# Cross-attention and routed feed-forward on one core: the routing weight loads on ScalarE's DMA queue, the weight differences in the middle head groups, the last reciprocals ahead of VectorE's closing work

## The chip, the core and the metric

The kernel runs on one core of a Trainium2 chip. Such a core has TensorE (PE, matrix products; its weight loads are listed apart as PEld), VectorE (DVE), ScalarE (ACT) and GpSimd (POOL), and SyncE (SP), which here only issues DMA transfers. Each engine works through its own instructions in order; they meet only at semaphores. DMA transfers are put into a queue by the engine that issues them: SP's queue and ScalarE's queue are the two that this kernel uses. SBUF is the on-chip memory, PSUM the banks that TensorE writes.

The metric is the time on the device in microseconds (us) of the whole program. Lower is better.

## The reference, cut to what matters

The inputs are x, 8 batches of 512 tokens by 512, and a context of 1601 rows by 128 for each batch, of which the causal mask leaves the first 512. Layer one is cross attention with 16 heads of 32:

```
x = x + Attention(layernorm(x), ctx, Wq, Wkv, Wout)     # causal softmax over keys
```

Layer two is a mixture of 8 experts whose weights are chosen per token and per output column:

```
logits = (h @ router_w.T + router_b).reshape(T, O, E)    # h = layernorm(x), O = 512, E = 8
w, sel = top_k(softmax(logits), 2);  w = w / sum(w)
c[t, e] = sum of w over the columns that chose e
x = x + sum_e c[t, e] * (h @ expert_w[e].T + expert_b[e])
```

Only differences of logits matter for the choice, so the kernel multiplies with 7 weight differences, router e minus router 0 (e = 1 to 7), rather than with 8 weights.

## The kernel before

All products of consequence are taken in three parts: each float32 operand is split into a high part (made on ScalarE, a rounding copy) and a low part (full minus high, on VectorE or GpSimd), and TensorE adds high*high, high*low and low*high. In the profile these are lines L264, L265 and L266.

The program has three stages. **Attention** walks over 8 batches; each has 4 head groups c = 0 to 3 of 4 heads, so 32 groups n = 0 to 31, and each group has 8 steps v = 0 to 7 (two heads and one block of keys each). TensorE runs `scores` of a later group (L608, L611), VectorE takes the row maxima (`maxima`, L1253), TensorE turns the maxima (L620), ScalarE and VectorE split them (`hi_shift` L949, `lo_shift` L1262), SP copies the two parts into rows 96 and 97 of the stacked operand `qk_st` (`rows`, L329), and `shifted_scores` (L638) repeats the score product with the maxima taken off. ScalarE takes the exponential (L997), GpSimd masks the diagonal block (L1696) and adds the blocks of keys up in `acc` (L1683, L1688), and TensorE forms the values (L651) and the sums (L663, L671); the sums of group n come in step v = 1 of group n + 1. In steps 1 to 3 VectorE takes their reciprocals (L1273), in step 4 it multiplies (`scaled`, L1279); ScalarE and GpSimd split the result into `oT_h` (L956) and `oT_l` (L1641). `project_out` for the batch before runs in groups c = 1 and 2; VectorE adds the residual (L1284) and SP stores it (L367). `stack` (L343) copies queries and keys of the group three ahead into `qk_st` by 12 transfers.

The **last batch** (groups 28 to 31) has no next batch to prepare. In it the routing weights are loaded into SBUF space that the projections no longer use, on SP's queue (L405, L407, L410; `w_raw`, 1 MB each; router 0 goes to slot 5), and VectorE subtracts router 0 in place (`diff_router`, L1358, 128x2048). The table PREPARED says in which (c, v) step each of the first five differences is taken. BIAS_STEPS does the same for five small instructions that split the router bias (7 partitions). SELECTED places GpSimd's work on `bias_sel` (L1727, L1732); its first step waits until the stacks of all 32 groups have landed.

Then comes the **tail of attention** (`epilogue` on each engine): the last output projection (`project_last`, 12 products of three for the three earlier groups, 4 of three for the last), whose last part waits for group 31's scaled outputs, the layer norm of the first token block (`stats2`, L1196; `deviation` on GpSimd, L1650 and L1652; `norm2`, L1210), its transposes (`turn_block`, L821) and their split (`hi_block` L1034, `lo_block` L1386), the last residual adds (L1289), and the split of the routing weights (`hi_router` L924 on ScalarE, `lo_router` L1398 on VectorE). Two differences (5 and 6) are taken on GpSimd (L1750), after `w_zero` and their weights have been loaded.

**Routing** then does 32 blocks of 128 tokens with 7 products of 12 matmuls each, and **experts** 32 blocks with 8. In the first expert block the weights are still being split (`hi_expert` L1093, `lo_expert` L1566). `put_c` (L1556 to L1561) lays out the coefficients of a block in `c_pad` and `turn_c` (L867) transposes them on TensorE, for block t + 1 after expert 3 of block t. `expert` (L1577) adds an expert's product to `xb` and so frees its PSUM bank.

The order on every engine is the order of the code: there is no scheduler. In the closing stretch the waits between engines set it.

## Time and profile before

| | |
|---|---|
| runs before | 2114.68, 2108.54 and 2114.58 us; median 2114.58 |
| profiled execution | 2109.79 us, its span 2108.1 us |
| TensorE busy | 2026.7 us, 96% of the span |
| VectorE, ScalarE, GpSimd busy | 70%, 48%, 40% |
| mean granted TensorE clock | 0.988 |

The profile's times are microseconds from the start of the span. A row of a timeline gives start, duration, engine, line, operation, output and inputs, the count of instructions merged in it, and in brackets the idle time before it with what ended it. A row of waits gives who waited for whom, the total, the number of waits and the longest. A row of the chain gives start, duration and what it is. A row of windows gives the stretch and its length, busy time of PE, PEld, DVE, ACT and POOL with counts, the granted TensorE clock as a share of full speed, the DMA share and GB/s. ("SPq" is SP's issuing of a transfer, not the transfer.)

Where the rows lie: group 29 (c = 1 of the last batch) runs from 622 to 642 us, group 30 from 648 to 666, group 31 from 666 to 685, the tail from 685 to 706, then routing until 1391.9 and the experts.

### The profile page before, as it was taken

What the parts mean: (1) busy time and instruction counts of PE and PEld (TensorE: products, weight loads), DVE (VectorE), ACT (ScalarE), POOL (GpSimd) and SP (SyncE); (2) the same over time, 40 slices, a digit from 0 to 9 for tenths busy, and PEclk for the clock granted to TensorE, in tenths of its full rate; (3) what the DMA queues carried; (4) which work ended last, traced back from release to release, by engine and by line L of the source; (5) the groups of instructions that cost most, each with busy time, mean ns of one, the idle gap of its engine ahead of it and who ended that gap; (6) DMA issues with size and microseconds to landing.
All of it is one profiled execution on the core that took longest, in us unless ns stands there. A gap on an engine that the chain in (4) does not pass through costs nothing.

```text
span 2108.1 us, 31621 instructions
## 1 busy us (share of the span) xinstructions
PE 2026.7 (96%) x10334; PEld 1564.7 (74%) x10384; DVE 1476.0 (70%) x2532; ACT 1005.4 (48%) x2030; POOL 852.7 (40%) x987
## 2 busy tenths in 40 slices
PE   4899999999997899999999999999999999999999
PEld 3666767766764677777777777778888888888887
DVE  4667767767666667777778777657877878778533
ACT  1454454454443346767676776733433334333300
POOL 3677677667667334435344345202311113111100
PEclk8999999999998999999999999999999999999999
DMA  5444544544544545455455355472322222322110
GB/s 154 104 106 125 141 116 115 144 117 112 129 108 165 185 161 204 161 193 184 162 177 204 150 190 188 156 269 81 109 95 75 78 92 93 107 80 75 60 40 31
DMA packets 99214, 275.82 MB, mean 131 GB/s; under 512 B 13435, under 2 KB 14480, under 8 KB 95030
## 3 DMA queue, kind: packets, MB, share of 16 engines
q1 hardware_dynamic: 94518, 216.16, 32.4%
q10 hardware_dynamic: 4608, 58.72, 8.1%
q8 instruction: 27, 0.44, 0.1%
q14 instruction: 61, 0.50, 0.1%
HBM read 131.67 MB, written 92.27 MB: 106 GB/s over the span
## 4 chain that ended last, share of the span: by engine, by line
PE 86%; DVE 7%; DMA 2%; issue 2%; POOL 1%; SPq 1%; ACT 1%; DVEq 0%; POOLq 0%; ACTq 0%
PE pair L264 21%; PE pair L266 20%; PE pair L265 20%; PE pair L608 4%; PE ps L264 3%; PE ps L651 3%; PE pair L638 3%; DVE nmax L1253 3%; PE ps L265 2%; PE ps L266 2%; PE pair L844 2%; PE pair L611 2%; DVE o_sb L1273 1%; PE ps L671 1%; DVE qk L1239 1%
## 5 line engine op out<-in xcount | busy, mean ns | idle before, releaser
L264 PE MATMUL pair<-w_h,hT 128*128 128x512 f32 x1920 | 797.4, 415 | 1.8 <-DVE w_l L1398 1.6
L266 PE MATMUL pair<-w_h,hT 128*128 128x512 f32 x1920 | 751.5, 391 | 0.0
L265 PE MATMUL pair<-w_l,hT 128*128 128x512 f32 x1920 | 747.6, 389 | 0.0
L1769 POOL TENSOR_TENSOR logits<-logits,second 128x512 f32<-128x512 f32 x224 | 298.4, 1367 | 608.1 <-DVE second L1456 607.8
L266 PEld LDWEIGHTS pair<-w_h,hT 128*128 128x128 f32 x1920 | 360.6, 188 | 80.3
L265 PEld LDWEIGHTS pair<-w_l,hT 128*128 128x128 f32 x1920 | 361.7, 188 | 74.6
L264 PEld LDWEIGHTS pair<-w_h,hT 128*128 128x128 f32 x1920 | 363.3, 189 | 69.6 <-issue 0.6
L997 ACT ACTIVATE pT<-pair,zero 128x1024 f32<-128x1024 f32 (+3 forms) x256 | 202.7, 793 | 258.9 <-PE pair L638 251.9
L1577 DVE SCALAR_TENSOR_TENSOR xb<-pair,c_now,xb 128x512 f32<-128x512 f32 x256 | 191.9, 750 | 189.2 <-PE pair L266 182.9
L1253 DVE TENSOR_REDUCE nmax<-pair 128x2 f32<-128x1024 f32 (+3 forms) x256 | 209.0, 816 | 150.4 <-PE pair L611 147.4
L1696 POOL TENSOR_SCALAR_AFFINE_SELECT pT<-pT 128x256 f32<-128x256 f32 x256 | 109.0, 427 | 147.0 <-ACT pT L997 146.3
L608 PE MATMUL pair<-qk_st 96*128 96x256 f32 (+3 forms) x512 | 135.5, 347 | 25.0 <-DVE nmax L1253 20.5
L1650 POOL TENSOR_TENSOR rstd<-moments,eps 128x1 f32<-128x1 f32 x64 | 33.0, 516 | 302.9 <-DVE moments L1206 268.3
L1510 DVE SCALAR_TENSOR_TENSOR scrap<-ps,w 128x512 bf16<-128x512 f32 x224 | 153.2, 684 | 0.0
L608 PEld LDWEIGHTS pair<-qk_st 96*128 96x128 f32 x512 | 88.7, 193 | 86.6 <-DVE nmax L1253 39.9
L1504 DVE SCALAR_TENSOR_TENSOR ps<-logits,ps 128x512 f32<-128x512 f32 x192 | 133.3, 694 | 17.0 <-DVE scrap L1510 0.5
L1061 ACT ACTIVATE over<-over 128x512 f32<-128x512 f32 x224 | 141.7, 633 | 7.0
L1058 ACT ACTIVATE junk<-over 128x512 bf16<-128x512 f32 x224 | 141.5, 632 | 7.1
L638 PE MATMUL pair<-qk_st 98*128 98x256 f32 (+3 forms) x512 | 135.1, 347 | 5.9 <-DMA qk_st<-nm_l 5.9
L1085 ACT ACTIVATE w<-tree 128x512 f32<-128x512 f32 x32 | 20.3, 633 | 238.0 <-DVE tree L1458 238.0
L1688 POOL TENSOR_TENSOR acc<-acc,pT 128x512 f32<-128x512 f32 (+1 forms) x124 | 128.8, 1039 | 10.3
L1053 ACT ACTIVATE over<-logits 128x512 f32<-128x512 f32 x224 | 129.6, 623 | 0.5
(164 smaller groups left out, 2877.4 us busy)
## 6 DMA issues: line engine op xcount, KB each, us to landing
logits<-lg_all ACTq DMA_DIRECT2D x32, 1792.0 KB, 7.8
qk_st<-qk SPq DMA_DIRECT2D x384, 128.0 KB, 2.3
lg_all<-ev_a SPq DMA_DIRECT2D x32, 768.0 KB, 6.0
lg_all<-ev_b SPq DMA_DIRECT2D x32, 768.0 KB, 3.2
xb<-x SPq DMA_DIRECT2D x64, 256.0 KB, 3.1
hT_all<-hT SPq DMA_DIRECT2D x32, 512.0 KB, 3.6
hT<-hT_all SPq DMA_DIRECT2D x32, 512.0 KB, 3.6
xt<-in_x SPq DMA_DIRECT2D x8, 1024.0 KB, 5.5
```

The lines of the kernel that those rows point to most:

```text
L264: pe.matmul(dst, lh, rh, start=start, stop=False)
L265: pe.matmul(dst, lh, rl, start=False, stop=False)
L266: return pe.matmul(dst, ll, rh, start=False, stop=stop)
L608: pe.matmul(s_ps[:, j, 0:w], qk_st[c][0:STACK, 0, hh, i * P:w], qk_st[c][0:STACK, 1, hh, 0:w], start=True, stop=False)
L638: mm = pe.matmul(dst[:, j, 0:w], qk_st[c][0:STACK + SHIFT_ROWS, 1, hh, kb * P:(kb + 1) * P], qk_st[c][0:STACK + SHIFT_ROWS, 0, hh, kb * P: ...
L997: act.activation(pT[kb][:, pair:pair + 2, :], src[:, :, 0:S - kb * P], ACT.Exp, bias=zero[:])\
L1058: act.activation(junk[:], over[j][:], ACT.Sign, accum_out=sign_sum[:, i, e:e + 1])\
L1061: act.activation(over[j][:], over[j][:], ACT.Tanh, scale=0.5, accum_out=tanh_sum[:, i, e:e + 1]).then_inc(s["first_step"], 1)
L1253: dve.tensor_reduce(nmax[:, c % 2, at:at + QB + 1:QB], s_ps[:, :, 0:(i + 1) * P], AX_X, ALU.max, negate=True)\
L1510: dve.scalar_tensor_tensor(scrap[:, e % 2, :], taken_ps[e % 2], 1.0, w2[:], ALU.min, ALU.mult, accum_out=c_taken[:, i, e - 1:e]).then_inc( ...
L1577: dve.scalar_tensor_tensor(xb[i][:], l_ps[e % 4], c_now[i][:, e:e + 1], xb[i][:], ALU.mult, ALU.add).then_inc(s["acc"], 1)
L1769: pool.tensor_tensor(logits[t % 2][:, e - 1, :], logits[t % 2][:, e - 1, :], second[:], ALU.subtract)\
```

## The change

The six routing weight loads and the two bias loads leave SP's queue. ScalarE issues them instead, one in each of six steps of the table LOADED, (0,6), (0,7), (1,0), (1,1), (1,3) and (1,5), behind that step's exponential. The five differences on VectorE move from steps (2,6), (2,7), (3,0), (3,5) and (3,6) to (1,2), (1,4), (2,2), (2,4) and (3,5), and the bias steps shift to other steps. In VectorE's epilogue the reciprocals and the scaling of group 31 stand first. On TensorE the transposes of the first token block come after two of the last four projection products, no longer before the four. `put_c` for block 1 runs before the first expert block instead of after its first expert.

```
@@ sync, last batch @@
-                    if not more and c == 0:
-                        sp.wait_ge(s["q_mm"], NB)
...
-                        sp.dma_start(w_raw[:, EARLY], r_v[:, 0]).then_inc(s["diff0_in"], 16)
-                        for e in range(1, EARLY - 1):
-                            sp.dma_start(w_raw[:, e - 1], r_v[:, e]).then_inc(s[f"diff{e}_in"], 16)
-                    if not more and c == 1:
-                        for e in range(EARLY - 1, EARLY + 1):
-                            sp.dma_start(w_raw[:, e - 1], r_v[:, e]).then_inc(s[f"diff{e}_in"], 16)
@@ tensor, epilogue @@
-                turn_block(0, 0)
                 for i in range(QB):
                     project_last(i, KC - 1)
+                    if i == 1:
+                        turn_block(0, 0)
@@ scalar @@
+            LOADED = ((0, 6), (0, 7), (1, 0), (1, 1), (1, 3), (1, 5))
+
+            def load_router(k):
+
+                if k == 0:
+                    act.wait_ge(s["q_mm"], NB)
+                    act.wait_ge(s["k_mm"], NB)
+                    act.wait_ge(s["v_mm"], B * QB)
+                    act.dma_start(w_raw[:, EARLY], r_v[:, 0]).then_inc(s["diff0_in"], 16)
+                else:
+                    act.dma_start(w_raw[:, k - 1], r_v[:, k]).then_inc(s[f"diff{k}_in"], 16)
+                if k == 1:
+                    act.dma_start(bias_raw[0:ND, :], router_b[1:NE, :]).then_inc(s["bias_in"], 16)
...
@@ vector @@
-            PREPARED = ((2, 6), (2, 7), (3, 0), (3, 5), (3, 6))
-            BIAS_STEPS = ((1, 4), (1, 5), (1, 6), (1, 7), (2, 5))
+            PREPARED = ((1, 2), (1, 4), (2, 2), (2, 4), (3, 5))
+            BIAS_STEPS = ((1, 5), (1, 6), (1, 7), (2, 0), (2, 6))
@@ vector, epilogue @@
                 dve.memset(bias_rows[:], 0.0).then_inc(s["bias_zero"], 1)
+                for v in DIVIDED:
+                    reciprocals(NB - 1, KC - 1, v, last_d_ps)
+                scaled(NB - 1, KC - 1, last_o_ps)
                 stats2(0, 0)
                 mean_variance(0, 0, "ln2")
                 lo_router(0)
                 norm2(0, 0)
-                for v in DIVIDED:
-                    reciprocals(NB - 1, KC - 1, v, last_d_ps)
-                scaled(NB - 1, KC - 1, last_o_ps)
                 lo_router(1)
@@ vector, experts @@
             put_c(0, 0)
+            dve.wait_ge(s["c_ok"], 2)
+            dve.wait_ge(s["c_put"], 1)
+            put_c(1, 1)
...
-                    if e == 0 and t + 1 < NT:
+                    if e == 0 and 0 < t < NT - 1:
```

VectorE in group 29 (c = 1 of the last batch), from the reciprocals of step 1 on, before; `o_sb` are the outputs of the group before, `xr` the residual, `nmax` the maxima:

```order
L1273 RECIPROCAL o_sb_89<-ps 128x176
L1253 TENSOR_REDUCE nmax<-pair 128x2
L1273 RECIPROCAL o_sb_89<-ps 128x176
L1284 TENSOR_TENSOR xr<-ps,xr 128x512
L1253 TENSOR_REDUCE nmax<-pair 128x2
L1273 RECIPROCAL o_sb_89<-ps 128x160
L1253 TENSOR_REDUCE nmax<-pair 128x2
L1279 TENSOR_TENSOR o_sb_89<-ps,o_sb_89 128x512
L1407 TENSOR_TENSOR bias_raw<-bias_raw,bias_zero_row 7x512
L1253 TENSOR_REDUCE nmax<-pair 128x2
```

The same place of the changed kernel, whose line numbers are four higher; `w_raw` are the routing weights:

```order
L1277 RECIPROCAL o_sb_89<-ps 128x176
L1257 TENSOR_REDUCE nmax<-pair 128x2
L1277 RECIPROCAL o_sb_89<-ps 128x176
L1362 TENSOR_TENSOR w_raw<-w_raw 128x2048
L1288 TENSOR_TENSOR xr<-ps,xr 128x512
L1257 TENSOR_REDUCE nmax<-pair 128x2
L1277 RECIPROCAL o_sb_89<-ps 128x160
L1257 TENSOR_REDUCE nmax<-pair 128x2
L1283 TENSOR_TENSOR o_sb_89<-ps,o_sb_89 128x512
L1362 TENSOR_TENSOR w_raw<-w_raw 128x2048
L1257 TENSOR_REDUCE nmax<-pair 128x2
```

One difference stands ahead of the residual add, a second one in the place of the first bias step, ahead of the last maxima. Group 30 gets two at the same places, with nothing taken out there.

VectorE's tail, from the scaling of group 30 to the second `lo_router`, before (`xb` is the first token block):

```order
L1279 TENSOR_TENSOR o_sb_91<-ps,o_sb_91 128x512
L1358 TENSOR_TENSOR w_raw<-w_raw 128x2048 x2
L1362 MEMSET bias_rows 128x256
L1196 BN_STATS stats<-xb_103 128x6
L1205 MEMSET turn 128x1
L1206 BN_AGGR moments<-stats 128x2
L1398 TENSOR_TENSOR w_l<-w_raw,w_h 128x2048
L1210 TENSOR_SCALAR xb_103<-xb_103,moments,rstd 128x512
L1273 RECIPROCAL o_sb_89<-ps 128x176 x2
L1273 RECIPROCAL o_sb_89<-ps 128x160
L1279 TENSOR_TENSOR o_sb_89<-ps,o_sb_89 128x512
L1398 TENSOR_TENSOR w_l<-w_raw,w_h 128x2048
```

The same tail of the changed kernel:

```order
L1283 TENSOR_TENSOR o_sb_91<-ps,o_sb_91 128x512
L1362 TENSOR_TENSOR w_raw<-w_raw 128x2048
L1366 MEMSET bias_rows 128x256
L1277 RECIPROCAL o_sb_89<-ps 128x176 x2
L1277 RECIPROCAL o_sb_89<-ps 128x160
L1283 TENSOR_TENSOR o_sb_89<-ps,o_sb_89 128x512
L1200 BN_STATS stats<-xb_103 128x6
L1209 MEMSET turn 128x1
L1210 BN_AGGR moments<-stats 128x2
L1402 TENSOR_TENSOR w_l<-w_raw,w_h 128x2048
L1214 TENSOR_SCALAR xb_103<-xb_103,moments,rstd 128x512
L1402 TENSOR_TENSOR w_l<-w_raw,w_h 128x2048
```

The reciprocals and the scaling of group 31 now stand ahead of the statistics, and one difference fewer stands ahead of both.

## Rows read from the trace of the kernel before

**Rows 1.** The waits of PE from 600 to 760 us, the five longest.
```profile
PE pair L264 <- POOL oT_l L1641: 6.8, 1, 6.8
PE pair L638 <- DMA qk_st<-nm_l: 5.9, 1, 5.9
PE ps L671 <- POOL acc L1688: 2.3, 1, 2.3
PE ps L651 <- POOL pT L1696: 2.0, 1, 2.0
PE ps L684 <- POOL pT L1696: 1.8, 1, 1.8
```

**Rows 2.** The timeline of SP, last batch.
```profile
631.50 1.89 SPq L407 DMA_DIRECT2D w_raw<-in_routerT  x3
633.44 2.71 SPq L367 DMA_DIRECT2D x<-xr  x1
```

**Rows 3.** The chain of waits, from 600 to 760 us.
```profile
633.44 11.56 DMA x<-xr
```

**Rows 4.** The timeline of PE, last batch and tail.
```profile
632.65 0.50 PE L264 MATMUL ps<-wo_h,oT_h 128*128 128x512 f32 x1 [0.73 <-DVE xr L1284]
...
652.61 0.83 PE L671 MATMUL ps<-acc,ones 128*32 128x384 f32 x8
...
673.19 1.50 PE L671 MATMUL ps<-acc,ones 128*32 128x384 f32 x8 [2.30 <-POOL acc L1688]
...
679.25 0.73 PE L638 MATMUL pair<-qk_st 98*128 98x256 f32 x4
...
685.24 0.50 PE L264 MATMUL pair<-wo_h,oT_h 128*128 128x512 f32 x1
...
700.97 0.77 PE L264 MATMUL pair<-wo_h,oT_h 128*128 128x512 f32 x1 [6.78 <-POOL oT_l L1641]
...
706.16 0.58 PE L264 MATMUL pair<-w_h,hT 128*128 128x512 f32 x1
```

**Rows 5.** The window of 5 us behind PE's idle time ahead of group 30.
```profile
645.00:650.00 5.00, 1.99 (x5) 1.62 (x6) 0.00 (x0) 0.73 (x1) 1.53 (x3) 0.50 0.56 151
```

**Rows 6.** The timeline of POOL, last batch and tail.
```profile
631.95 0.85 POOL L1727 MEMSET bias_sel<- 128x896 bf16 x1 [7.09 <-DMA qk_st<-qk]
...
645.89 0.72 POOL L1688 TENSOR_TENSOR acc<-acc,pT 128x256 f32<-128x256 f32 x1
...
661.30 1.28 POOL L1688 TENSOR_TENSOR acc<-acc,pT 128x512 f32<-128x512 f32 x1
...
663.48 3.34 POOL L1688 TENSOR_TENSOR acc<-acc,pT 128x512 f32<-128x512 f32 x1
...
690.12 2.15 POOL L1650 TENSOR_TENSOR rstd<-moments,eps 128x1 f32<-128x1 f32 x1 [4.40 <-DVE moments L1206]
```

**Rows 7.** The timeline of DVE, last batch and tail.
```profile
635.04 0.95 DVE L1407 TENSOR_TENSOR bias_raw<-bias_raw,bias_zero_row 7x512 f32<-7x512 f32 x1
...
663.40 2.27 DVE L1358 TENSOR_TENSOR w_raw<-w_raw 128x2048 f32<-128x2048 f32 x1
...
689.12 0.70 DVE L1196 BATCH_NORM_STATS2 stats<-xb 128x6 f32<-128x512 f32 x1 [5.37 <-DMA xb<-x]
...
693.39 3.38 DVE L1273 RECIPROCAL o_sb<-ps 128x176 f32<-128x176 f32 x3
...
712.99 5.58 DVE L1210 TENSOR_SCALAR xb<-xb,moments,rstd 128x512 f32<-128x512 f32 x1 [0.72 <-POOL rstd L1652]
```

**Rows 8.** The timeline of PE, first expert block.
```profile
1405.67 0.47 PE L867 MATMUL ps<-ident,c_pad 128*128 128x128 f32 x1 [2.39 <-DVE c_pad L1561]
...
1415.97 0.47 PE L264 MATMUL pair<-w_h,hT 128*128 128x512 f32 x1 [0.17 <-DVE xb L1577]
```

**Rows 9.** The timelines of SP and DVE, first expert block.
```profile
1405.53 0.38 SPq L487 DMA_DIRECT2D w_raw<-in_expertT  x1
...
1412.87 2.29 DVE L1566 TENSOR_TENSOR w_l<-w_raw,w_h 128x2048 fp32r<-128x2048 f32 x1 [3.73 <-ACT w_h L1093]
```

More of the change, by code:

```diff
@@ L310, in over_batches @@
             epilogue()
+        r_v = routerT.rearrange("(c p) e o -> p e c o", p=P)
         block = ctx.enter_context(nc.Block())
@@ L394, in body @@
                         load_x(b + 2)
-                    if not more and c == 0:
-                        sp.wait_ge(s["q_mm"], NB)
-                        sp.wait_ge(s["k_mm"], NB)
-                        sp.wait_ge(s["v_mm"], B * QB)
-                        sp.dma_start(bias_raw[0:ND, :], router_b[1:NE, :]).then_inc(s["bias_in"], 16)
-                        sp.dma_start(bias_zero_row[0:ND, :], router_b[0:1, :].broadcast_to([ND, O]))\
-                            .then_inc(s["bias_in"], 16)
-                        sp.dma_start(w_raw[:, EARLY], r_v[:, 0]).then_inc(s["diff0_in"], 16)
-                        for e in range(1, EARLY - 1):
-                            sp.dma_start(w_raw[:, e - 1], r_v[:, e]).then_inc(s[f"diff{e}_in"], 16)
-                    if not more and c == 1:
-                        for e in range(EARLY - 1, EARLY + 1):
-                            sp.dma_start(w_raw[:, e - 1], r_v[:, e]).then_inc(s[f"diff{e}_in"], 16)
             def load_block(t, i, name):
@@ L448, in epilogue @@
                     sp.wait_ge(s[f"x1_out{k}"], B * QB // 2 * 16)
-            r_v = routerT.rearrange("(c p) e o -> p e c o", p=P)
             e_v = expertT.rearrange("(c p) e o -> p e c o", p=P)
@@ L924, in hi_router @@
                 act.activation(w_h[:, k], w_raw[:, k], ACT.Copy).then_inc(s["fw_hi"], 1)
+            LOADED = ((0, 6), (0, 7), (1, 0), (1, 1), (1, 3), (1, 5))
[9 more added lines that the diff above has]
+                    act.dma_start(bias_raw[0:ND, :], router_b[1:NE, :]).then_inc(s["bias_in"], 16)
+                    act.dma_start(bias_zero_row[0:ND, :], router_b[0:1, :].broadcast_to([ND, O]))\
+                        .then_inc(s["bias_in"], 16)
             def hi_weight(dst, src, name):
@@ L1007, in body @@
                             hi_of(n + AHEAD, QH, "q", 1)
+                        if last and (c, v) in LOADED:
+                            load_router(LOADED.index((c, v)))
                         if c == 0 and more:
```

## The prediction

> **What bounds the kernel now.** I read the page's busy times first: TensorE is busy 96% of the span. In routing and experts nothing but its own matmuls matters, so the change can act only on the few stretches where it waits. The list of its waits around the end of attention shows them [rows 1]: 6.8 us for GpSimd's `oT_l`, 5.9 for the rows of maxima, 2.3 and 2.0 for GpSimd's sums and masks, 1.8 for a mask again; together 18.8 us. Then the timelines, to see what stands behind each wait, and the windows for TensorE's clock: in the 5.9 us wait it falls to 0.50, the lower of its two levels (1.2 GHz) [rows 5], and after the two waits for GpSimd eight matmuls take 1.50 us that took 0.83 in the group before [rows 4].
>
> Each wait's cause is one row further back. The 5.9 us: SP has put four 1 MB weight loads ahead of the residual store; the store, issued at 633.44, lands 11.56 us later [rows 2, 3], SP waits for it before it reloads that buffer, and only then, at 645, the rows of group 30 can go. The 2.3 and 2.0: a VectorE difference (2.27 us) starts at 663.40, GpSimd's add at 663.48 takes 3.34 us, and the same add without it took 1.28 [rows 6, 7]. So a difference holds GpSimd up by 2.06 us. The 6.8: group 31's reciprocals start at 693.39 [rows 7], though their sums are done by 685.24 [rows 4]; ahead of them in VectorE's order stand the statistics, whose token block arrives at 689.12, a `lo_router` and a `norm2`.
>
> **Group 29: the loads leave SP's queue.** The store now meets no weight loads in its own queue, and the rows of maxima go out when they are ready. The 5.9 us wait goes, and with it the slow clock behind it. What is late next is GpSimd. It waits for the last stack until 631.95 and is then busy without a break until its last add ends at 645.89 + 0.72 = 646.6 [rows 6]. Two differences now fall into that stretch: 2 x 2.06 = 4.1, so 650.7. The stack shares the DMA engines with ScalarE's loads; I add 0.5 us (bounds: 0, and 11.6, the store's landing, if it stood behind them all). The sums of group 29 then start at 651.2 instead of 652.61 [rows 4]. VectorE's own delay is 2.27 and 2.27 - 0.95 for the bias step that made room [rows 7], 3.6 us, plus some waiting for GpSimd; it puts TensorE at those sums at about 649, covered by GpSimd's 651.2. Term: **-1.4 us**. ScalarE's eight issues cost some half a microsecond each (1.89 us for three on SP [rows 2]) and stand in gaps of about 1 to 2 us between exponentials; if its queue pushed back as in the store's 2.71 us [rows 2], it could be 2 us in one step, which GpSimd's lag hides as well.
>
> **Group 30: two differences in the middle.** VectorE has no idle time from step 1 to step 5 there; TensorE already waited 0.73 us for the residual add in the same step of group 29 [rows 4]. So both differences lie on the path: 2 x 2.27 = 4.5, and 0.5 for differences that find a GpSimd instruction running. Bounds: 4.5 and, if each waits for a whole 1.28 us add, 7.1. **+5.0 us**. In return none stands at the end of group 30: the waits of 2.0 and 2.3 [rows 1] go. **-4.3 us**. The sums of group 30 start at 673.19 - 1.4 + 5.0 - 4.3 = 672.5.
>
> Here the Trainium skill bears (SBUF — State Buffer, Who interferes with whom): a VectorE instruction with two inputs in SBUF and a GpSimd instruction that reads SBUF exclude each other entirely, and whichever issued first goes on. The trace agrees on both sides: 3.34 against 1.28 for GpSimd, and a 5.58 us `norm2` on VectorE that met GpSimd's long subtraction [rows 6, 7]. By that rule a moved difference costs the same wherever GpSimd is busy; if the two merely shared bandwidth, group 29 would give some 2 us more.
>
> **Group 31.** Before, the clock was low from 673.19: eight L671 took 1.50 against 0.83 at full speed [rows 4], and the 6.06 us from there to 679.25 are about 3.6 at full clock. **-2.4 us**. One difference is left in step 5; it still holds GpSimd's last masks, so most of the 1.8 us wait stays: **-0.1**. The last projection starts at 685.24 - 3.2 = 682.0.
>
> **The tail.** All from there. Reciprocals 682.1 to 685.5 (3.38 [rows 7]), scaling to 686.2. The token block arrives three microseconds earlier too, as its issue hangs on group 30's `oT_l`: 686.2. Statistics and variance take 0.9 us, GpSimd's deviation 2.15 beside a `lo_router` [rows 6] and a short power 0.55: 689.9; only then comes GpSimd's `oT_l`, 1.3 us: 691.2. TensorE has worked on the other 36 matmuls to 690.3 and waits 0.9 us, not 6.8. At full clock 12 matmuls take 2.8 instead of the 5.2 us from 700.97 to 706.16 [rows 4]. But the transposes now stand between them (0.6), and behind them the split of the block on ScalarE and VectorE and a residual add, 0.9 us beyond TensorE's own end. Routing starts at 691.2 + 2.8 + 0.6 + 0.9 = 695.5, not 706.16: -10.7. Its fifth product hangs on VectorE's `norm2` and `lo_router`, and these on the residual adds, which end 9.8 us earlier. So attention gives **-9.8 us** in all, of which the tail has 6.6.
>
> **The early put_c.** TensorE waits 2.39 us for `c_pad` at 1405.67 and then runs slowly, 8 matmuls at 0.43 instead of 0.23 us apart: 4.0 us in all (the two paces are those of the 12 matmuls above). Both go. But expert 7 starts at 1415.97 behind VectorE's `xb` add, which stands behind the last `lo_expert` (1412.87 + 2.29), whose weights were only requested at 1405.53 [rows 8, 9]. None of that moves. The 4.0 us turn into a wait ahead of expert 7, and a wait so long brings the lower clock behind it, now uncovered: 8 x 0.2 = **+1.7 us** (bounds 0 and 2.5).
>
> **Sum.** -9.8 + 1.7 = -8.1 us. Against the profiled execution's own 2109.8 this is 2101.7; against the median 2114.6 it is 2106.5. The runs of before differ by 6 us among themselves, so I take a value between, 2104.
>
> **The rivals.**
> *A. The loads hold up the last stack.* ScalarE's first four loads are issued while SP stacks group 31. If the DMA engines serve them first, the stack lands late by about the 11 us that four loads took [rows 3], GpSimd's `bias_sel` step waits for it [rows 6], and its backlog sets group 29's sums us for us: -8.1 + 11 = +3, 2112.8 from the profiled time and up to 2117.5 from the median, slower than before. It decides from 8.1 us of delay on. For it: the store's 11.56 us. Against: the store stood in the same queue. The Trainium skill (DMA: Bandwidth & Descriptors, Queues, rings and completion order) says that each DMA engine takes turns between queues, packet by packet; by it the stack would only share the engines with the loads, and rival A would come to almost nothing. No row of this trace shows two such queues at once.
> *B. The middle costs more.* If each of group 30's two differences first waits for a GpSimd add (2 x 1.28), and TensorE's stalls of 3 us there bring the lower clock (2 x 1.6), the sum is -8.1 + 5.8 = -2.3: 2107.5, or 2112 from the median. For it: VectorE has no slack; against: a slow TensorE is partly hidden behind VectorE there.
> *C. GpSimd is no hindrance and the clock holds.* Then group 29 gives 2.6 us more, and expert 7's wait costs nothing (1.7): -12.4, 2097.4. For it: waits of 1.8 and 2.0 us left the clock alone; against: the rows of the lock.
>
> **Chances.** Forecast 0.48 (its own range -5 to -11), B 0.25, C 0.20, A 0.07. Less than 0.3%, 6.3 us, can't be told from no change here. Faster by more: four fifths of the forecast's, nearly all of C's and a little of B's, 0.6. Within: the rest of the forecast's, most of B's, most of A's, 0.35. Slower by more: 0.05. The range 2096 to 2112 takes in C with a microsecond to spare and B from either base.
>
> **What would show it.** In the changed profile: no wait for `qk_st<-nm_l`; a wait of 1 to 3 us at the sums of group 29 for GpSimd; new waits of 2 to 3 us for the residual add (L1288) and the maxima (L1257); the 2.0 and 2.3 us waits for GpSimd gone at the end of group 30; the wait for `oT_l` about 1 us; routing's first product 10 to 11 us earlier; a 4 us wait ahead of expert 7 and none for `c_pad`. Wrong would be: a late GpSimd memset of `bias_sel` (A), or group 30's sums later than in the kernel before (B).

## The result, and the profile after

The forecast was 2104 us (2096 to 2112), 8.1 us less than before. Measured: a median of 2116.63 us (2112.47 to 2119.66, 17 runs) against 2112.77 us of the kernel before (2108.54 to 2114.75, 17 runs). The ratio is 1.002, with a 95% interval of 1.0013 to 1.0028: slower, by some 4 us. The prediction was wrong in sign and in size.

The profiled execution took 2119.66 us, its span 2117.9 against 2108.1 before. From its page, busy times and then the DMA queues (packets, MB, share of 16 engines' span):

```profile
PE 2037.6 (96%) x10334; PEld 1571.8 (74%) x10384; DVE 1479.5 (70%) x2532; ACT 1005.8 (47%) x2030; POOL 849.9 (40%) x987
...
q1 hardware_dynamic: 91322, 209.84, 31.2%
q10 hardware_dynamic: 7804, 65.04, 9.0%
```

The loads did move: ScalarE's queue (q10) carries 65.04 MB instead of 58.72.

**4.6 of the 9.8 us between the two spans have nothing to do with the change.** The sums of group 27 (the last ones before any changed code) start at 608.09 us before and at 612.70 after. The windows where this arises, of the kernel after (columns: stretch, length, busy time of PE, PEld, DVE, ACT and POOL, then TensorE's granted clock):

```profile
100.00:110.00 10.00, 10.00 (x66) 6.60 (x65) 5.68 (x10) 3.77 (x5) 5.16 (x14) 0.70 0.65 150
110.00:120.00 10.00, 8.96 (x45) 5.53 (x43) 7.34 (x12) 6.51 (x11) 8.50 (x10) 0.83 0.05 11
```

The kernel before has a granted clock of 1.00 in both windows, in the same code. So all that follows is measured from group 27's sums. Where the milestones stand from there, in us, each read from the first matmul of its kind in TensorE's timeline (in step 1 of a group TensorE sums the group before), the memset from GpSimd's:

| milestone | before | after | p1 | p2 | p3 | p4 | q3 | r1 | r2 | r3 | s1 |
|---|---|---|---|---|---|---|---|---|---|---|---|
| GpSimd's memset of `bias_sel` | 23.9 | 32.8 | 32.8 | 31.3 | 32.1 | 31.2 | 28.3 | 31.6 | 24.1 | 29.2 | 22.5 |
| group 28's sums | 17.9 | 20.0 | 21.2 | 21.4 | 22.5 | 20.1 | 17.9 | 22.3 | 17.9 | 17.9 | 17.9 |
| group 29's sums | 44.5 | 47.9 | 46.9 | 45.6 | 51.2 | 47.8 | 44.2 | 49.4 | 45.0 | 42.9 | 44.2 |
| group 30's sums | 65.1 | 70.5 | 67.5 | 67.6 | 71.9 | 73.2 | 64.8 | 73.4 | 65.5 | 65.8 | 65.0 |
| last projection | 77.1 | 79.8 | 79.9 | 79.6 | 81.2 | 82.5 | 77.0 | 82.7 | 77.6 | 78.4 | 78.3 |
| routing, product 1 | 98.1 | 93.3 | 100.1 | 93.1 | 102.1 | 96.0 | 90.5 | 96.2 | 91.2 | 91.9 | 91.8 |
| routing, product 5 | 112.8 | 113.0 | 114.8 | 112.8 | 116.8 | 115.6 | 110.2 | 112.6 | 107.6 | 108.3 | 104.2 |
| routing, product 6 | 115.8 | 118.3 | 117.8 | 118.1 | 119.8 | 119.9 | 115.7 | 116.9 | 112.7 | 112.7 | 109.8 |
| experts | 783.8 | 786.3 | 785.8 | 786.0 | 787.8 | 787.8 | 783.6 | 784.9 | 780.7 | 780.7 | 779.2 |
| expert block 2 | 810.9 | 815.5 | 813.1 | 812.1 | 816.6 | 813.3 | 812.4 | 815.6 | 808.3 | 808.0 | 805.6 |
| end | 1500.0 | 1505.2 | 1502.2 | 1501.1 | 1505.6 | 1502.4 | 1501.5 | 1504.6 | 1497.3 | 1497.1 | 1494.5 |

(p1 to s1 are the experiments below.) The loss from group 27 on is 5.2 us, near the 3.9 us of the medians. TensorE's waits in the end of attention, kernel after, 600 to 770 us (total, times, longest), which answer to [rows 1]:

```profile
PE ps L264 <- DVE xr L1288: 5.9, 2, 2.9
PE ps L807 <- DVE xb L1214: 3.1, 1, 3.1
PE ps L605 <- DVE nmax L1257: 2.6, 2, 1.5
PE pair L830 <- ACT w_h L910: 2.2, 1, 2.2
PE pair L623 <- DMA qk_st<-nm_l: 2.1, 1, 2.1
PE pair L264 <- DVE w_l L1402: 1.4, 1, 1.4
...
PE pair L264 <- POOL oT_l L1648: 0.8, 1, 0.8
```

The 6.8 us for `oT_l` are 0.8, the 5.9 us for rows are gone, and the 2.3 and 2.0 us for GpSimd in [rows 1] are no longer among the long ones. But others came: two of 2.9 us for the residual add; 2.1 us for rows, one group earlier than the 5.9 had been; and three in routing's first block (L807, L830, `w_l`), 6.7 us together, where the kernel before waits 0.37 and 1.61.

The issues of ScalarE's and SP's queues around the last stack (start, length):

```profile
623.33 0.45 ACTq L920 DMA_DIRECT2D w_raw<-in_routerT  x1
625.31 0.39 ACTq L922 DMA_DIRECT2D w_raw<-in_routerT  x1
...
630.18 0.39 ACTq L922 DMA_DIRECT2D w_raw<-in_routerT  x1
632.12 0.41 ACTq L922 DMA_DIRECT2D w_raw<-in_routerT  x1
637.10 0.37 ACTq L922 DMA_DIRECT2D w_raw<-in_routerT  x1
```
```profile
624.27 0.57 SPq L331 DMA_DIRECT2D qk_st<-nm_h  x1
624.88 0.59 SPq L331 DMA_DIRECT2D qk_st<-nm_l  x1
625.64 8.07 SPq L345 DMA_DIRECT2D qk_st<-qk  x12
641.56 0.35 SPq L369 DMA_DIRECT2D x<-xr  x1
647.48 0.33 SPq L365 DMA_DIRECT2D xr<-in_x  x1
```

What came of it, first in the chain of waits, then on GpSimd, then on TensorE:

```profile
633.11 12.26 DMA qk_st<-qk
```
```profile
645.49 0.85 POOL L1734 MEMSET bias_sel<- 128x896 bf16 x1 [13.71 <-DMA qk_st<-qk]
```
```profile
629.41 0.73 PE L623 MATMUL pair<-qk_st 98*128 98x512 f32 x2 [2.08 <-DMA qk_st<-nm_l]
...
641.59 0.60 PE L264 MATMUL ps<-wo_h,oT_h 128*128 128x512 f32 x1 [2.93 <-DVE xr L1288]
...
669.49 0.80 PE L264 MATMUL ps<-wo_h,oT_h 128*128 128x512 f32 x1 [2.92 <-DVE xr L1288]
```

The last piece of the stack, issued at 633.11, lands 12.26 us later. GpSimd's memset comes 32.8 us behind group 27's sums, where it was 23.9 [rows 6]: 8.9 us late, and I had given it 0.5. The residual store now stands behind no load in its own queue, and SP still goes on only 5.9 us after it (641.56 to 647.48; 11.56 in [rows 3]); the median of these stores is 2.1 us.

**This one profile shows the middle milder than most.** Nine kernels here (after, p1 to p4, q2, q4, q5, r1) issue the loads at these early steps, and each has a wait of 1.97 to 2.36 us for group 29's rows. In after and p4 the granted clock stayed at 1.00 behind it; in the other seven it fell to 0.50. Their group 28's sums stand at 21.2 to 22.5, those of after and p4 at 20.0 and 20.1, and those of every kernel without early loads at 17.9 (s1 17.8). The mean of the nine is 21.5, so this place costs 3.6 us in the mean and not 2.1.

### The profile page after: what moved, and what is told of

Read it like the earlier page. It is cut to its first block, busy times and chain, and to the rows that moved or that the text cites. A ratio compares the mean times of both kernels' runs of the same rounds, so it can differ in the third digit from the quotient of the medians.

```text
span 2117.9 us, 31622 instructions
## 1 busy us (share of the span) xinstructions
PE 2037.6 (96%) x10334; PEld 1571.8 (74%) x10384; DVE 1479.5 (70%) x2532; ACT 1005.8 (47%) x2030; POOL 849.9 (40%) x987
## 3 DMA queue, kind: packets, MB, share of 16 engines
q1 hardware_dynamic: 91322, 209.84, 31.2%
q10 hardware_dynamic: 7804, 65.04, 9.0%
## 4 chain that ended last, share of the span: by engine, by line
PE 86%; DVE 7%; DMA 2%; issue 2%; POOL 1%; SPq 1%; ACT 0%; DVEq 0%; POOLq 0%; ACTq 0%
PE pair L264 21%; PE pair L266 20%; PE pair L265 20%; PE pair L593 4%; PE ps L636 3%; PE ps L264 3%; PE pair L623 3%; DVE nmax L1257 3%; PE ps L265 2%; PE ps L266 2%; PE pair L830 2%; PE pair L596 2%; DVE o_sb L1277 1%; DVE qk L1243 1%; PE ps L656 1%
```

## The experiments

Each ratio is that to the kernel before on the same chip, with its 95% interval. First the loads were made alone, and then each other part undone by itself. Diffs are against the kernel after, where nothing else is said.

### p1: the loads alone

The kernel before, with the loads on ScalarE and nothing else of the change.

```diff
-PREPARED = ((1, 2), (1, 4), (2, 2), (2, 4), (3, 5))
-BIAS_STEPS = ((1, 5), (1, 6), (1, 7), (2, 0), (2, 6))
+PREPARED = ((2, 6), (2, 7), (3, 0), (3, 5), (3, 6))
+BIAS_STEPS = ((1, 4), (1, 5), (1, 6), (1, 7), (2, 5))
...  and the tail and put_c as in the kernel before
```

> The kernel before with one part of the change, the loads on ScalarE's queue. Distances are counted from the sums of group 27 (before: sums of group 29 at +44.5, last projection at +77.2, routing at +98.1). Theory (loads and last stack share the DMA engines, GpSimd's bias_sel waits for the stack): the wait of 5.9 us for the rows goes, but bias_sel starts 7 to 9 us later, group 29's sums stand at +47 to +49, the last projection at +80, and the kernel is 2 to 5 us slower than before. Rival (only the moved differences cost anything): bias_sel on time, sums of group 29 at +39 to +41, the kernel 5 us faster than before.

Measured: 2112.89 us, ratio 1.0008 [0.9997, 1.0019]: by the time alone no difference from before, where 2 to 5 us were expected. What follows is read from its profile. The loads alone bring GpSimd's memset to 32.8 us and group 28's sums to 21.2 instead of 17.9:

```profile
626.52 0.73 PE L623 MATMUL pair<-qk_st 98*128 98x512 f32 x2 [1.97 <-DMA qk_st<-nm_l]
...
643.96 1.28 PE L636 MATMUL ps<-pT,v_sb 128*32 128x512 f32 x8 [2.22 <-POOL pT L1699]
...
655.98 0.43 PE L636 MATMUL ps<-pT,v_sb 128*32 128x128 f32 x8 [1.90 <-POOL pT L1699]
```

So the new wait for group 29's own rows and the late stack both belong to the loads. The 5.9 us wait is gone, and waits for GpSimd's masks stand in its place. The last projection comes 2.8 us later than before. Three kernels (before, r2, s1) share all code up to that point and have it at 77.1, 77.6 and 78.3, mean 77.7; p1 and p2 have 79.9 and 79.6. So the early loads cost about 2.1 us in the mean of profiles.

### p2: the old middle

After, with the two tables `PREPARED` and `BIAS_STEPS` of before (the diff of p1's first four lines).

> The changed kernel with the differences and bias steps back at their old places, all else as changed. Theory: group 29's sums stay at +47 to +49 (changed kernel +47.9), since the stack is late without the differences too; group 30's waits for GpSimd of 2.0 and 2.3 us come back; the last projection at +79 to +81; time within 2 us of the changed kernel. Rival (the moved differences are the whole loss): sums of group 29 at +40, time 7 us under the changed kernel.

Measured: 2114.48 us, ratio 1.0013 [1.0003, 1.0024]. The last projection is at 79.6, that of after at 79.8. But six kernels here (after, p3, p4, q4, q5, r1) share all code up to that point, and theirs lies at 79.8 to 82.9, mean 81.9. p1 and p2, with the old middle behind early loads, have 79.9 and 79.6. The moved differences thus cost 2.2 us in the mean of profiles, and a single profile can't show it; the intervals of the times overlap.

### p3: the old tail

```diff
-                for v in DIVIDED: reciprocals(...)      # ahead of stats2
-                scaled(NB - 1, KC - 1, last_o_ps)
                 stats2(0, 0)
                 mean_variance(0, 0, "ln2")
                 lo_router(0)
                 norm2(0, 0)
+                for v in DIVIDED: reciprocals(...)
+                scaled(NB - 1, KC - 1, last_o_ps)
...  turn_block ahead of the loop
```

> The changed kernel with VectorE's and TensorE's tail in the old order. Theory: last projection at +79.8 as changed, then the 6.8 us wait for oT_l is back and routing starts at +100 to +101 instead of +93.3; the fifth product follows 14.7 us later at about +115.5 instead of +113.1; so 2 to 3 us slower than the changed kernel. Rival (the tail's gain is taken back entirely by the weight chain): fifth product at +113, no difference in time.

Measured: 2116.9 us, ratio 1.0023 [1.0014, 1.0032], no different from after. Its own trace:

```profile
706.77 0.77 PE L264 MATMUL pair<-wo_h,oT_h 128*128 128x512 f32 x1 [6.77 <-POOL oT_l L1647]
```

The 6.8 us wait is back. Expected were 2 to 3 us more than after; the rival named with it, that the weight chain takes the tail's gain back, came true. From the last projection to product 1 it takes 20.9 us, as before (21.0); after takes 13.5. Yet at product 6 p3 stands at 119.8 and after at 118.3, and 1.4 of these 1.5 us they were apart at the last projection already. The tail's gain exists and is gone within six products. It is so in every pair: product 1 to product 6 takes 17.7 us in the three kernels with the old tail (before, p1, p3), and 23.9 to 25.2 in the five that have the new tail and nothing done about GpSimd (after, p2, p4, q2, q3).

p3's profile also shows what the wait for group 29's rows costs where the clock falls behind it; the two matmuls took 0.73 us in after. Below them the window of 5 us behind it, with the granted clock at 0.50:

```profile
626.71 1.22 PE L623 MATMUL pair<-qk_st 98*128 98x512 f32 x2 [2.19 <-DMA qk_st<-nm_l]
```
```profile
627.00:632.00 5.00, 5.00 (x23) 3.41 (x26) 0.96 (x1) 1.94 (x2) 0.41 (x1) 0.50 1.04 256
```

### p4: the old put_c

```diff
-            dve.wait_ge(s["c_ok"], 2)
-            dve.wait_ge(s["c_put"], 1)
-            put_c(1, 1)
...
-                    if e == 0 and 0 < t < NT - 1:
+                    if e == 0 and t + 1 < NT:
```

> The changed kernel with put_c of block 1 after the first expert, as before. Theory: TensorE waits 2.4 us for c_pad and not 4.6 us ahead of expert 7, expert 7 starts no later, and 1.6 us of slow clock behind it go: 1.6 us faster than the changed kernel. Rival (the early put_c gains what it removes): 2.4 us slower than the changed kernel.

Measured: 2114.42 us, ratio 1.0013 [1.0003, 1.0023]. From expert 7 to the second block p4 takes 3.0 us, as before, and after 4.6. Ahead of expert 7, after and then p4:

```profile
1423.57 0.77 PE L264 MATMUL pair<-w_h,hT 128*128 128x512 f32 x1 [4.62 <-DVE xb L1581]
```
```profile
1407.83 0.33 PE L853 MATMUL ps<-ident,c_pad 128*128 128x128 f32 x1 [0.75 <-DVE c_pad L1565]
...
1418.11 0.47 PE L264 MATMUL pair<-w_h,hT 128*128 128x512 f32 x1 [1.75 <-DVE xb L1581]
```

The early `put_c` turns the wait for `c_pad` into a longer one, 4.6 us, and the matmul behind it takes 0.77 us instead of 0.47. In these two profiles that is 1.6 us behind expert 7. The whole first expert block takes 28.6 us in the mean of the eight kernels with the early `put_c` and 26.9 in that of the six without (p4 25.5, after 29.2). The lower clock is not certain: p2 has the early `put_c` too, waits 3.30 us ahead of expert 7, keeps a clock of 1.00 and takes 3.1 us to the second block. p4's time doesn't part from that of after.

### q2: the masks later

Was the late stack harmful through `bias_sel` and the masks that stand behind it in GpSimd's order? Here they don't stand behind it.

```diff
-SELECTED = ((1, 0), (1, 2), (1, 4), (2, 0))
+SELECTED = ((1, 7), (2, 1), (2, 3), (2, 7))
```

> The changed kernel with GpSimd's four bias_sel steps moved to (1,7), (2,1), (2,3), (2,7), so that no mask or add of group 29 stands behind the wait for the last stack. If that wait is what carries the late stack to TensorE, GpSimd keeps pace with the exponentials, group 29's sums come as soon as VectorE's two differences let TensorE reach them, at +44 to +46 from the sums of group 27 instead of +47.9, and the kernel is 2 to 4 us faster than the changed one. Rival (VectorE's differences alone set group 29, GpSimd's lag is covered): sums of group 29 stay at +47 to +48, time unchanged.

Measured: 2115.85 us, ratio 1.003 [1.0017, 1.0042]. The 2 to 4 us that were expected didn't come. Group 29's sums come at 46.6 instead of 47.9, but the last projection at 80.0 (after 79.8). Against the mean of the six kernels with the middle of after (49.2 and 81.9) the two are 2.6 and 1.9 us earlier, so profiles leave room for a gain that the time doesn't show. The two waits of 2.9 us for the residual add behind VectorE's differences are there unchanged: GpSimd's lag alone is not what holds group 30 up.

### q3: the loads later

```diff
-            LOADED = ((0, 6), (0, 7), (1, 0), (1, 1), (1, 3), (1, 5))
+            LOADED = ((1, 2), (1, 3), (1, 4), (1, 5), (1, 7), (2, 1))
...  PREPARED and BIAS_STEPS as in the kernel before
```

> The changed kernel with the differences at their old places and ScalarE's loads later, at (1,2), (1,3), (1,4), (1,5), (1,7), (2,1), behind the last stack. Theory (loads beside the stack delay it and the rows of group 29): bias_sel starts at +24 as in the kernel before, not +31 to +33; group 28's sums are back at +18; group 29's at +39 to +41; the last projection 4 to 6 us earlier than with the early loads (+79.6). Rival (any load on ScalarE's queue costs this much wherever it stands): last projection at +79 again.

Measured: 2110.75 us, ratio 1.0004 [0.9995, 1.0013]. Group 28's sums are back at 17.9 and the last projection at 77.0. That is where the kernel before has it, and not 4 to 6 us before p2's, as expected. GpSimd's memset is still late, 28.3 instead of 23.9, since the first load (630.46) is issued while SP still stacks (622.77 to 631.83). The other hindrance is in VectorE's rows: the bias step now waits for its load, in the place of the 5.9 us wait.

```profile
641.48 0.69 DVE L1411 TENSOR_TENSOR bias_raw<-bias_raw,bias_zero_row 7x512 f32<-7x512 f32 x1 [4.61 <-DMA bias_zero_row<-in_router_b]
```

Product 1 comes at 90.5, 7.6 us before that of the kernel before, and product 6 at 115.7, where before has 115.8. So with a middle that costs nothing against before, the whole gain of the tail is given back between product 1 and product 6: 25.2 us against 17.7 before.

### q4 and q5: where the gain goes

The kernel after, GpSimd in routing's first block:

```profile
707.43 4.62 POOL L1757 TENSOR_TENSOR w_raw<-w_raw,w_zero 128x2048 f32<-128x2048 f32 x1 [5.75 <-DMA w_raw<-in_routerT]
...
717.84 4.56 POOL L1757 TENSOR_TENSOR w_raw<-w_raw,w_zero 128x2048 f32<-128x2048 f32 x1
```

VectorE, and TensorE:

```profile
707.56 6.63 DVE L1402 TENSOR_TENSOR w_l<-w_raw,w_h 128x2048 fp32r<-128x2048 f32 x1
...
717.91 5.52 DVE L1214 TENSOR_SCALAR xb<-xb,moments,rstd 128x512 f32<-128x512 f32 x1 [0.72 <-POOL rstd L1659]
```
```profile
714.29 0.38 PE L830 MATMUL pair<-bias_rows,bias_sel 128*128 128x512 bf16 x1 [2.19 <-ACT w_h L910]
...
723.49 0.89 PE L807 MATMUL ps<-ident,xb 128*128 128x128 f32 x4 [3.06 <-DVE xb L1214]
725.75 0.99 PE L264 MATMUL pair<-w_h,hT 128*128 128x512 f32 x1 [1.37 <-DVE w_l L1402]
727.39 0.63 PE L264 MATMUL pair<-w_h,hT 128*128 128x512 f32 x1
```

GpSimd's first subtraction hangs on a load that SP issues at 699.22 and 699.72, behind token blocks and bias rows. In the kernel before, the tail was late and the subtraction ran inside it, 700.78 to 705.33, ahead of the third `lo_router` (706.99, 2.28 us). Now routing starts earlier and the load does not: the subtraction starts at 707.43, the third `lo_router` at 707.56, and it ends 2.1 us after GpSimd is through: 6.63 us, as if it had begun only then. The next weight's `lo_router`, the norm and the fifth product follow late. q4 makes GpSimd wait for the third `lo_router`; q5 also makes the second subtraction wait for `norm2`, which met it before the change too [rows 7].

```diff
                 if k == EARLY:
+                    pool.wait_ge(s["fw_lo"], 3)
                     pool.wait_ge(s["base_in"], 16)
...  q5 also:
             deviation(1, 1, "ln2")
+            pool.wait_ge(s["hn_ok"], 2)
             diff_router(EARLY + 1)
```

> The changed kernel with one wait more on GpSimd: its first subtraction of router 0 (4.6 us) only starts once VectorE's third lo_router is done. Theory (the subtraction shuts VectorE out, lo_router takes 6.6 us instead of 2.3 and the third routing product waits): the 2.2 us wait ahead of the third product goes, norm2 of the second block is still held up by the second subtraction, and the sixth product stands at +116 to +118 instead of +118.3: 0 to 2 us faster. Rival (the weights' DMA is the limit): nothing changes.

> As the one before, and GpSimd's second subtraction also waits until norm2 of the second token block is done. Theory: both meetings of VectorE and GpSimd go, norm2 takes 0.6 instead of 5.5 us, the fifth product starts at +105 to +107 instead of +113.0 and the clock stays high behind it, sixth at +108 to +111: 7 us faster than the changed kernel, 3 us faster than the one before. Rival (the last routing weights come too late then): a wait of 3 us or more ahead of the seventh product, and little gain.

Measured: q4 2113.61 us, ratio 1.0018 [1.0009, 1.0027]; q5 2118.96 us, 1.0035 [1.0022, 1.0047]. VectorE in q4:

```profile
707.18 2.28 DVE L1402 TENSOR_TENSOR w_l<-w_raw,w_h 128x2048 fp32r<-128x2048 f32 x1
710.20 6.11 DVE L1402 TENSOR_TENSOR w_l<-w_raw,w_h 128x2048 fp32r<-128x2048 f32 x1
```

The third `lo_router` is short again (the meeting is the cause of its length), but the next one meets the subtraction instead, and product 6 is at 120.1. From product 1 to product 6 it takes 23.7 us, after 25.0, and the times don't part. This wait mostly chooses which VectorE instruction pays. In q5 the norm takes 0.55 us instead of 5.52, but ScalarE's copy of the seventh weight, now later, stands ahead of its copies of the logits:

```profile
725.83 0.99 PE L264 MATMUL pair<-w_h,hT 128*128 128x512 f32 x1 [6.77 <-ACT ev_a L1115]
```

So the time saved at the norm is lost again, and more, at a wait of 6.77 us: product 1 to product 6 takes 26.4 us, and the 7 us expected over after didn't come.

### r1, r2, r3: the load earlier

If the meeting is the cause, the cure is the load, not the wait. r1 is after, with SP's issues of `w_zero` and of weight 6 ahead of the second token block:

```diff
                 load_block(0, 0, "xb_in")
+                sp.wait_ge(s["summed"], NB)
+                sp.dma_start(w_zero[:], r_v[:, 0]).then_inc(s["base_in"], 16)
+                sp.wait_ge(s["fw_diff"], EARLY)
+                sp.dma_start(w_raw[:, 5], r_v[:, 6]).then_inc(s["diff6_in"], 16)
                 load_block(1, 1, "xb_in")
```

> The changed kernel with one thing more: SP requests router 0 (w_zero) and router 6, which GpSimd's first subtraction needs, right behind the first token block instead of behind the second block and the bias rows. Theory (that subtraction, held back to 707.4 by its load, runs into VectorE's third lo_router): it now starts 3 to 5 us earlier, while VectorE reads PSUM in lo_block and the residual adds; lo_router takes 2.3 and not 6.6 us, the 2.2 us wait ahead of the third product goes, fifth product at +108 to +110 (changed kernel +113.0), sixth at +111 to +113 (+118.3), and the kernel is 4 to 7 us faster than the changed one. Rival (the chain norm2, lo_router is as late as it is for other reasons): fifth product at +113 again.

r2 is the kernel before with this edit and the new tail alone (the minus lines of p3's diff in place of its plus lines): no loads on ScalarE, no moved differences, the old `put_c`.

> The kernel before with only the new tail (reciprocals first, transposes between the last products) and those two earlier loads; loads on SP's queue, differences and put_c as before. Theory: last projection at +77.2 as before, routing at +90.5, fifth product at +106, sixth at +109 (before +115.8): 5 to 7 us faster than the kernel before. Rival (the tail cannot be kept, the chain takes it all back): no difference from the kernel before.

r3 is r2 with q3's late loads on ScalarE, the bias steps moved behind their load.

> As the one before, and the routing weights on ScalarE's queue at (1,2) to (2,1), behind the last stack, with the bias steps late enough, (2,0) to (2,6), not to wait for their load, as they did for 4.6 us at (1,4) in the run with the late loads. Theory: the 5.9 us wait for the rows of group 30 goes at last, since neither the store nor the bias holds them; group 29's sums at +40 to +42 instead of +44.5; 2 to 4 us faster than the one before. Rival (the loads slow the residual store on the shared DMA engines just as much in another queue): +44 again and no gain over it.

Measured: r1 2113.94 us, ratio 1.0016 [1.0007, 1.0025]; r2 2108.37 us, 0.9983 [0.9974, 0.9992]; r3 2109.82 us, 0.9993 [0.9984, 1.0002]. GpSimd and VectorE in r1:

```profile
703.50 4.72 POOL L1757 TENSOR_TENSOR w_raw<-w_raw,w_zero 128x2048 f32<-128x2048 f32 x1 [2.23 <-DMA w_raw<-in_routerT]
```
```profile
707.13 3.25 DVE L1402 TENSOR_TENSOR w_l<-w_raw,w_h 128x2048 fp32r<-128x2048 f32 x1
```

The meeting costs 1 us instead of 4.4, and product 1 to product 6 takes 20.7 us instead of 25.0. The times of r1 and after don't part clearly, since r1's profile has a late middle (82.7; the clock fell behind its wait for the rows). r2 keeps part of the gain: product 6 at 112.7, 3.1 us before that of the kernel before, the end 2.7 earlier, and the medians 2.9 apart; 5 to 7 us were expected. From product 1 to product 6 r2 takes 21.5 us, q3 with the same tail and the load not moved 25.2, the kernel before 17.7. r3 says what the loads are worth on ScalarE's queue when the rows and the bias no longer collide with them (the stack still does, its memset is at 29.2): group 29's sums come at 42.9 instead of 45.0 in r2, the last projection at 78.4 instead of 77.6, product 6 at 112.7 in both. Nothing, in this place, where 2 to 4 us were expected.

### s1: r2 and the norm first

r2 with the second subtraction behind `norm2`, and ScalarE's copy of the seventh weight behind its third copy of logits, which q5 had lacked.

```diff
+            pool.wait_ge(s["hn_ok"], 2)
             diff_router(EARLY + 1)
...
-                for k in range(4, ND):
+                for k in range(4, ND - 1):
                     hi_router(k)
...
                     copy_logits(t, k)
+                    if t == 0 and k == 2:
+                        hi_router(ND - 1)
```

> The kernel before with the new tail and the earlier loads of router 0 and router 6 (the run that was 0.17% faster), and with norm2 of the second block ahead of GpSimd's second subtraction (one wait) and ScalarE's last hi_router behind the copy of the third routing product, not ahead of all copies. Theory (the weight chain loses time where VectorE and GpSimd shut each other out, and where ScalarE's copies queue behind a split that waits for GpSimd): norm2 takes 0.6 instead of 5.5 us, the sixth product starts at +108 to +110 instead of +112.4 (before: +115.8), and the kernel is 2 to 4 us faster than without these two edits, 5 to 7 us faster than the kernel before. Rival (the sum of VectorE's and GpSimd's exclusive work is what counts, its order is not): sixth or seventh product as late as before, no gain beyond the 0.17%.

Measured: 2106.7 us (12 runs) against 2110.36, ratio 0.9979 [0.997, 0.9988]: faster than the kernel before and, by the ratios, than after. Over r2 (0.9983) the time shows no gain that is clear of noise; 2 to 4 us were expected. In the profile product 6 is at 109.8, 6.0 us before that of the kernel before, and product 1 to product 6 takes 18.0 us, near the 17.7 of before. VectorE:

```profile
714.93 0.55 DVE L1213 TENSOR_SCALAR xb<-xb,moments,rstd 128x512 f32<-128x512 f32 x1 [0.72 <-POOL rstd L1655]
715.40 11.09 DVE L1401 TENSOR_TENSOR w_l<-w_raw,w_h 128x2048 fp32r<-128x2048 f32 x3
```

GpSimd:

```profile
715.56 6.58 POOL L1753 TENSOR_TENSOR w_raw<-w_raw,w_zero 128x2048 f32<-128x2048 f32 x1 [0.66 <-DVE xb L1213]
```

The three last `lo_router` pay now (11.09 us instead of 6.68 in after), and so does the subtraction; TensorE needs their weights later than it needs the norm. But the subtraction's own result is needed at product 6:

```profile
724.38 0.59 PE L845 MATMUL pair<-bias_rows,bias_sel 128*128 128x512 bf16 x1 [2.42 <-ACT w_h L925]
724.41 0.99 PE L264 MATMUL pair<-w_h,hT 128*128 128x512 f32 x1
```

Behind this wait the clock is low again and product 6 to product 7 takes 4.4 us instead of 3.0. At the experts s1 is 4.6 us ahead of the kernel before and 1.5 ahead of r2.

## Why the prediction was wrong

Its steps beside what they came to, each as the change of the stretch between two milestones:

| step | forecast | measured |
|---|---|---|
| up to group 28's sums | 0 | +2.1 |
| group 29 | -1.4 | +1.3 |
| group 30 | +0.7 | +2.0 |
| group 31 to the last projection | -2.5 | -2.7 |
| tail, to routing's product 1 | -7.5 | -7.5 |
| product 1 to product 6 | +0.9 | +7.3 |
| routing's rest | 0 | 0.0 |
| first expert block, put_c | +1.7 | +2.1 |
| the rest | 0 | +0.6 |
| sum | -8.1 | +5.2 |

The largest miss, 6.4 of these 13.3 us, is that from product 1 to product 6; the next, 4.8, is the path to group 29's sums.

**The step that failed most: "attention gives -9.8 us".** It followed routing's fifth product back to `norm2` and `lo_router` and these to the residual adds, 9.8 us earlier, and took their lengths as they were. It didn't ask what GpSimd does in that stretch in the new order. [rows 7] had `norm2` at 5.58 us beside a subtraction, so the price of a meeting was in sight; the load on which the first subtraction hangs was not followed. Shown by r1 (the load earlier: 4.3 us of the 7.3 back), by q4 (the third `lo_router` 2.28 us), and by r2 against q3 (21.5 us instead of 25.2). The meeting at `norm2` makes up the rest: with it gone as well, s1 takes 18.0. A part is TensorE's clock behind the waits: the matmul at 727.39 takes 0.63 us, the granted clock is 0.50 in the window from 725 to 730, and product 5 to product 6 takes 5.2 us instead of 3.0. By product 5 the chain had cost +5.0.

The Trainium skill's rule on the shared port (SBUF — State Buffer, Who interferes with whom: a VectorE instruction with two inputs in SBUF and a GpSimd one that reads SBUF exclude each other, the first issued goes on) agrees with these rows, 6.63 against 2.28 us. The 5.58 us of `norm2`, which the prediction put beside that rule, is no example of it: its row has one large input. That `norm2` stands still beside the subtraction is shown by s1, where it takes 0.55 us without it. I had weighed the rule in the middle groups, and not in routing's first block, where it decided.

**"The stack shares the DMA engines with ScalarE's loads; I add 0.5 us"** was 8.9. This is rival A's mechanism, to which I gave 0.07. Its sign in the trace is there (a late memset), its price is not: it was to pass through in full. p1 has the loads alone and loses 2.8 us by the last projection (2.1 in the mean of profiles); q2 takes the masks from behind the memset and has its last projection where after has it. So most of the 8.9 us seems to be covered by other waits. The row of the store, 11.56 us, had been set aside because the store stood in the same queue as the loads. In after the loads stand in the other one and SP still waits 5.9 us. The Trainium skill (DMA: Bandwidth & Descriptors, Queues, rings and completion order) has each DMA engine take turns between queues, packet by packet, and I had read from it that the stack would lose almost nothing. No row shows the turns themselves; but that reading is wrong by the rows: with the DMA engines filled (share 1.04 to 1.06 from 630 to 645 us), the last piece of the stack lands 12.26 us after its issue. The measurement decides.

**A wait that I had not looked for:** the rows of group 29 themselves, issued at 624.27 beside the first load (623.33), 2.08 us late on TensorE. It stands in all nine kernels with the early loads (1.97 to 2.36) and in none with the loads later or on SP's queue. This is the +2.1 ahead of group 28's sums, and with the clock that fell behind it in seven of the nine it is 3.6 in their mean. The prediction had no term for it.

**Group 30: two differences in the middle** cost more than 5.0, since the two waits of 2.9 us for the residual add are each followed by the lower clock: matmuls of 0.63 and 0.80 us instead of 0.40 (granted clock 0.68 from 640 to 645, 0.50 from 670 to 675). That was rival B, and it is in the trace (group 30 +2.0 instead of +0.7, group 29 +1.3). In the mean of profiles the moved differences cost 2.2 us by the last projection, which no time here confirms by itself.

**The signs that I had named.** Rival A's (a late memset) and rival B's (group 30's sums later, 70.5 after 65.1) both came. Routing's first product was to be 10 to 11 us earlier and was 4.8. The wait of 1 to 3 us for GpSimd at group 29's sums was 0.43: the chain of waits still runs through GpSimd there, but TensorE itself came so late that little of it showed.

**What was right.** The tail: -7.5 forecast and measured, `oT_l` 0.9 forecast and 0.83 measured; p3 undoes it and has the 6.77 us wait again. Group 31: the two waits for GpSimd are gone, and with them the slow matmuls (683.21, 0.83 us; 1.50 in [rows 4]). `put_c`: a wait of 4.62 us ahead of expert 7 and none for `c_pad`; +1.6 of the +2.1 lie between expert 7 and the second block, and p4 has them back. (The prediction's 8 x 0.2 is 1.6, not 1.7.) That the clock falls there is partly luck of the execution: in p2 it didn't.

**What stays open.** How much the moved differences cost in the median (0 to 3.3 us in single profiles, 2.2 in their mean). How p1's 2.8 us divide between the late stack and the late rows of group 29: q3 and r3 have the memset 4.4 and 5.3 us late, no late rows, and the last projection at 77.0 and 78.4, where before, r2 and s1 have 77.1 to 78.3. So they lose nothing against before, but the end of the 5.9 us wait gives them nothing either, and whether the late stack takes that gain isn't shown; a stack 7 to 9 us late without late rows was not made. Why waits of the same length left the clock alone in some executions and not in others; and the clock of 0.70 and 0.83 from 100 to 120 us, which came in one execution of unchanged code.

## What to carry to other kernels

A chain that is made earlier is early only as far as all its inputs are: list what each of its engines waits for, the loads of the helper engine too, and look what they run into at their new times. A wait added to keep two engines apart mostly picks who pays (q4, q5); start the blocked work sooner (r1, r2), or let the work pay that is needed last (s1, so far as its profile shows). A profile is one execution: where kernels share their code up to a point, compare that point over all of them before you put a difference of 2 us down to a change. And a transfer moved to another queue still runs on the same DMA engines: before moving it, look which small transfers with a waiter are issued in the next 10 us, in any queue.

## What the runs showed of the hardware

- **1 MB loads in ScalarE's queue delayed small transfers of SP's queue.** The last stack's last piece landed 12.26 us after its issue (the page's median for such a piece is 2.3), and the rows of maxima held TensorE up by 2.08 us (1.97 to 2.36 in all nine kernels with the early loads).
- **VectorE and GpSimd held each other up by whole instructions, in both directions.** `lo_router` 2.28 to 6.63 us, `norm2` 0.55 to 5.52, the same `lo_router` 3.25 when it met only the end of a subtraction; GpSimd's subtraction 4.56 to 6.58 in s1. There three `lo_router` take 11.09 us instead of 6.68, and the 4.4 more is about the length of the one subtraction beside them (4.56). VectorE's residual adds, which read one operand from PSUM, were not held up: in r1 two of them take 1.28 us beside the subtraction, as in after without one.
- **TensorE's clock.** Behind the idle 2.9 us at 669.49 the granted clock was 0.50, its lower level (1.2 GHz), from 670 to 675; behind the 4.62 us ahead of expert 7 it was 0.81 from 1425 to 1430; behind the 3.30 us ahead of expert 7 in p2 it was 1.00. Behind the 2.08 us wait for rows in after the matmuls kept their length (0.73 us for two at 629.41, 0.83 for the sums at 632.68), and so they did in p4; behind the wait of 2.19 us for the same rows in p3 the clock was 0.50 from 627 to 632. The length of the wait alone doesn't decide it.
